# Global attention: where the results are normalised and where the row maxima are split and turned

## The reference

```
scores = q @ k.T / sqrt(8)          # per head, 1024 x 1024
attn   = softmax(scores, axis=-1)
out    = attn @ v
```

## Time and profile before

| what | value |
|---|---|
| three runs | 3819.56, 3825.5, 3826.06 us (median 3825.5) |
| profiled execution, device time | 3821.91 us |
| its span, first to last instruction | 3820.1 us |
| mean granted TensorE clock | 0.987 |
| busy share of the whole span | PE 96%, DVE 84%, ACT 75%, POOL 63% |
| global attention within the span | about 61 us to 750 us |

### The profile page before, as it was taken

How to read it: one execution, slowest core, us unless ns; L and a number is a source line. 1 busy time by engine, 2 the same in 40 slices (tenths; PEclk the granted TensorE clock), 3 DMA queues, 4 the chain that set the end, 5 groups by cost and what they waited for, 6 DMA issues and landing times. The chain is left out here.

```text
span 3820.1 us, 161411 instructions
## 1 busy us (share of the span) xinstructions
PE 3661.5 (96%) x70604; PEld 2660.4 (70%) x70604; DVE 3217.1 (84%) x4678; ACT 2863.7 (75%) x5074; POOL 2397.6 (63%) x1986
## 2 busy tenths in 40 slices
PE   6999999959999999999999999999999999999997
PEld 2222222247888888888888888888888888888885
DVE  7999999668888888888888888888888888888884
ACT  3888888857777777777777777777777777777774
POOL 3100000077777777878777777778777777778783
PEclk8999999989999999999999999999999999999999
DMA  3110000034444344433444344444444443444432
GB/s 117 38 39 21 20 22 18 7 95 109 110 112 106 104 122 113 111 107 104 119 115 112 105 106 116 120 110 105 106 116 116 111 106 105 127 117 109 108 105 57
DMA packets 202568, 360.17 MB, mean 94 GB/s; under 512 B 35522, under 2 KB 74054, under 8 KB 201542
## 3 DMA queue, kind: packets, MB, share of 16 engines
q1 hardware_dynamic: 201802, 348.76, 34.3%
HBM read 236.73 MB, written 111.67 MB: 91 GB/s over the span
## 5 line engine op out<-in xcount | busy, mean ns | idle before, releaser
L1202 POOL TENSOR_TENSOR T<-T 128x1024 f32<-128x1024 f32 x384 | 909.2, 2380 | 25.9 <-DVE T L1681 25.1
L1220 POOL TENSOR_TENSOR T<-T,rn 128x1024 f32<-128x1024 f32 x384 | 732.0, 1907 | 27.1 <-POOL rn L1213 0.4
L1292 PE MATMUL PA<-Wqkv,XS 128*128 128x512 f32 x2304 | 633.4, 410 | 11.4 <-DVE XS L1642 8.2
L787 ACT ACTIVATE E<-p_low 128x512 f32<-128x512 f32 x1024 | 556.2, 597 | 114.6 <-PE p_low L637 100.5
L716 DVE TENSOR_REDUCE negmax<-p_max 128x1 f32<-128x1024 f32 x512 | 588.9, 1215 | 19.7 <-PE p_max L616 19.7
L1292 PEld LDWEIGHTS PA<-Wqkv,XS 128*128 128x128 f32 x2304 | 414.7, 193 | 81.9 <-DVE XS L1642 11.2
L1689 DVE TENSOR_REDUCE ss<-SQ 128x32 f32<-128x2048 f32 x192 | 436.9, 2275 | 0.0
L1368 PE MATMUL PB<-ET,VW 64*64 64x32 f32 x24576 | 399.6, 220 | 16.8 <-DVE T L1681 8.8
L1368 PEld LDWEIGHTS PB<-ET,VW 64*64 64x64 f32 x24576 | 377.5, 135 | 54.8 <-DVE T L1681 28.6
L1320 PE MATMUL PD<-ident,T 128*128 128x128 f32 x3072 | 409.5, 276 | 6.3 <-POOL T L1220 5.3
L1381 PEld LDWEIGHTS PD<-Wo,OT 128*128 128x128 f32 x3072 | 365.9, 192 | 61.3 <-issue 61.1
(11 more groups left out here) (165 smaller groups left out, 6718.8 us busy)
## 6 DMA issues: line engine op xcount, KB each, us to landing
VW<-v_rows SPq DMA_DIRECT2D x768, 256.0 KB, 4.5
v_rows<-Vs SPq DMA_DIRECT2D x192, 512.0 KB, 6.0
Wraw<-in_Wqkv SPq DMA_DIRECT2D x40, 192.0 KB, 5.1
QA<-parts_q SPq DMA_DIRECT2D x384, 16.0 KB
KA<-parts_k SPq DMA_DIRECT2D x192, 32.0 KB
parts_q<-AO SPq DMA_DIRECT2D x8, 384.0 KB, 2.7
parts_k<-AO SPq DMA_DIRECT2D x8, 384.0 KB, 3.3
Wo<-in_Wo SPq DMA_DIRECT2D x12, 256.0 KB, 4.8
```

The costliest lines, as they stand in the source:

```text
L787: act.activation(E[:, s % 4, c, :], p_s[:, (64 * g + i) % NS, :], ACT.Exp, scale=DH ** -0.5)\
L1202: pool.tensor_tensor(out=t_, in0=t_, in1=T2[:, i * HALF:(i + 1) * HALF], op=ALU.add).then_inc(ad.sem, 1)
L1220: pool.tensor_tensor(out=t_, in0=t_, in1=rn[:, p, i * LH:(i + 1) * LH].unsqueeze(2).broadcast_to([P, LH, LD]), op=ALU.mult).then_inc(no.se ...
L1292: mm = pe.matmul(pair[:, half, :], XS[:, b, i, 1:P + 1], Wqkv[:, l % 2, j, lo:lo + 512], start=(k == 0), stop=(k == 2))
```

## The change

- `max_rows`: DVE now makes the two bfloat16 parts from the columns (`nmc`, 128 x 16 each), directly behind the sixteenth reduction. PE transposes both parts in bfloat16 into one bank of the score ring, and ACT copies the 16 x 256 rows to `nmb`. SP's DMAs wait for ACT.
- `result`: PE transposes into a bank of the score ring. ACT copies the bank (128 x 512) back to OE; POOL raises the sums to the power -1 and multiplies into AO. `result_copy` now waits for POOL's product of the group before (s_ao).
- The three score banks are numbered by `ring`: scores, rows and results in one list. p_max holds units alone.
- Rows move from steps 5 and 13 to 4 and 12, between scores 1 and 2; units from five steps of two to four (24 are done ahead of group 0, where there were 22); `late` goes.
- At the start PE's wait for `s_lo` and `s_va` of the opening stands ahead of `max_rows(0, 0)`.

```diff
     def units(g, s):
-        if s < 5:
-            return [(g, 1, 6 + 2 * s + i) for i in range(2)]
+        if s < 4:
+            return [(g, 1, 8 + 2 * s + i) for i in range(2)]
         if g + 1 == NG:
             return []
-        if s < 13:
-            return [(g + 1, 0, 2 * (s - 5) + i) for i in range(2)]
-        return [(g + 1, 1, 2 * (s - 13) + i) for i in range(2)]
+        if s < 12:
+            return [(g + 1, 0, 2 * (s - 4) + i) for i in range(2)]
+        return [(g + 1, 1, 2 * (s - 12) + i) for i in range(2)]
...
     def on_pool(pool):
+        def result(g, qh):
+            b, hg = divmod(g, HG)
+            o = OE[:, qh, :].rearrange("p (q c w) -> p q c w", q=4, w=VW)
+            pool.wait_ge(s_ex.sem, s_ex.at(RING["result", g, qh]))
+            pool.tensor_tensor(out=rsum[:, qh, :, :], in0=o[:, :, :, DH], in1=minus[:, :, :], op=ALU.pow)\
+                .then_inc(s_rc.sem, 1)
+            pool.wait_ge(s_rc.sem, s_rc.at(g, qh + 1))
...
+            pool.tensor_tensor(out=a[:, :, hg, :, :], in0=o[:, :, :, 0:DH],
+                               in1=rsum[:, qh, :, :].unsqueeze(3).broadcast_to([P, 4, GH, DH]),
+                               op=ALU.mult).then_inc(s_ao.sem, 1)
...
             pool.tensor_copy(VG[:, g % 2, :, :, 0:DH + 1], VA[:, g // HG, :, heads(g), :]).then_inc(s_vg.sem, 1)
+            if g >= 2:
+                result(g - 2, 1)
+            if g >= 1:
+                result(g - 1, 0)
...
+        result(NG - 2, 1)
+        result(NG - 1, 0)
+        result(NG - 1, 1)
...
     def on_pe(pe):
         def max_rows(g, qh):
-            k = TURN["rows", g, qh]
-            pe.wait_ge(s_mr.sem, s_mr.at(k - 1))
-            pe.transpose(p_max[0:GH * 4, k % 2, 0:P], negmax[:, qh, :, :].rearrange("p c q -> p (c q)"),
-                         ident[:, :]).then_inc(s_mx.sem, 1)
+            n = RING["rows", g, qh]
+            pe.wait_ge(s_mb.sem, s_mb.at(g, qh + 1))
+            if n >= NS:
+                pe.wait_ge(s_ex.sem, s_ex.at(n - NS))
+            for j in range(2):
+                mm = pe.transpose(p_s[0:GH * 4, n % NS, :].bitcast(BF16)[:, j * P:(j + 1) * P], nmc[:, qh, j, :],
+                                  w["ident_b"][:, :])
+            mm.then_inc(s_st.sem, 1)
...
         def result(g, qh):
-            k = TURN["result", g, qh]
+            n = RING["result", g, qh]
             pe.wait_ge(s_oe.sem, s_oe.at(g, qh + 1))
-            pe.wait_ge(s_mr.sem, s_mr.at(k - 2))
+            pe.wait_ge(s_ex.sem, s_ex.at(n - NS))
             for qt in range(4):
-                mm = pe.transpose(p_max[:, k % 2, qt * P:(qt + 1) * P], OE[:, qh, qt * P:(qt + 1) * P], ident[:, :])
-            mm.then_inc(s_mx.sem, 1)
+                mm = pe.transpose(p_s[:, n % NS, qt * P:(qt + 1) * P], OE[:, qh, qt * P:(qt + 1) * P], ident[:, :])
+            mm.then_inc(s_st.sem, 1)
...
     def on_dve(dve):
         def max_rows(g, qh):
-            k = TURN["rows", g, qh]
-            dve.wait_ge(s_mx.sem, s_mx.at(k))
+            dve.wait_ge(s_mr.sem, s_mr.at(TURN["unit", g, qh, HU - 1]))
             if g > 0:
-                dve.wait_ge(s_md.sem, s_md.at(g - 1, 64 * (qh + 1)))
-            rows = p_max[0:GH * 4, k % 2, 0:P]
-            dve.tensor_copy(nmb[:, qh, 0, :], rows).then_inc(s_mb.sem, 1)
-            dve.wait_ge(s_mb.sem, s_mb.at(g, qh + 1))
-            dve.tensor_tensor(out=nmb[:, qh, 1, :], in0=rows, in1=nmb[:, qh, 0, :],
-                              op=ALU.subtract).then_inc(s_mr.sem, 1)
+                dve.wait_ge(s_st.sem, s_st.at(RING["rows", g - 1, qh]))
+            columns = negmax[:, qh, :, :].rearrange("p c q -> p (c q)")
+            dve.tensor_copy(nmc[:, qh, 0, :], columns).then_inc(s_nc.sem, 1)
+            dve.wait_ge(s_nc.sem, s_nc.at(g, qh + 1))
+            dve.tensor_tensor(out=nmc[:, qh, 1, :], in0=columns, in1=nmc[:, qh, 0, :],
+                              op=ALU.subtract).then_inc(s_mb.sem, 1)
...
     def on_act(act):
         def result_copy(g, qh):
             act.wait_ge(s_pv.sem, s_pv.at(g, 8 * (qh + 1)))
             if g > 0:
-                act.wait_ge(s_mx.sem, s_mx.at(TURN["result", g - 1, qh]))
+                act.wait_ge(s_ao.sem, s_ao.at(g - 1, qh + 1))
...
+        def max_rows(g, qh):
+            n = RING["rows", g, qh]
+            act.wait_ge(s_st.sem, s_st.at(n))
+            if g > 0:
+                act.wait_ge(s_md.sem, s_md.at(g - 1, 64 * (qh + 1)))
+            act.activation(nmb[:, qh, :, :].rearrange("r j n -> r (j n)"),
+                           p_s[0:GH * 4, n % NS, :].bitcast(BF16)[:, 0:2 * P], ACT.Copy).then_inc(s_ex.sem, 1)
+
+        def result(g, qh):
+            n = RING["result", g, qh]
+            act.wait_ge(s_st.sem, s_st.at(n))
+            act.activation(OE[:, qh, :], p_s[:, n % NS, :], ACT.Copy).then_inc(s_ex.sem, 1)
+
+        max_rows(0, 0)
         for g in range(NG):
             for s in range(16):
                 for c in range(GH):
-                    i = 4 * s + c
-                    act.wait_ge(s_st.sem, s_st.at(g, i + 1))
+                    if s == 4 and c == 2:
+                        max_rows(g, 1)
+                    if s == 12 and c == 2 and g + 1 < NG:
+                        max_rows(g + 1, 0)
...
+                if s == 3 and g > 0:
+                    result(g - 1, 1)
+                if s == 11:
+                    result(g, 0)
...
         result_copy(NG - 1, 1)
+        result(NG - 1, 1)
```

More of the change, by code:

```diff
@@ L473, in global_attention @@
     s_mr = m.count("s_mr")
+    s_nc = m.count("s_nc", 2)
     s_mb = m.count("s_mb", 2)
     s_md = m.count("s_md", 128)
-    s_st = m.count("s_st", 64)
-    s_ex = m.count("s_ex", 64)
+    s_st = m.count("s_st")
+    s_ex = m.count("s_ex")
+    s_ao = m.count("s_ao", 2)
+    s_mi = m.count("s_mi")
     s_pv = m.count("s_pv", 16)
@@ L523, in turns, with ring, add @@
                 todo = units(g, s)
[L524 to L527, removed]
+                for u in todo:
+                    add("unit", *u)
+        return at
+    TURN = turns()
+    def ring():
+        at = {}
+        def add(kind, *key):
+            at[(kind, *key)] = len(at)
+        add("rows", 0, 0)
+        for g in range(NG):
+            for s in range(16):
+                add("score", g, s, 0)
+                add("score", g, s, 1)
+                if s == 4:
                     add("rows", g, 1)
-                if s == 13 and g + 1 < NG:
+                if s == 12 and g + 1 < NG:
                     add("rows", g + 1, 0)
[L531 to L534, removed]
+                add("score", g, s, 2)
+                add("score", g, s, 3)
                 if s == 3 and g > 0:
@@ L540, in turns @@
         return at
-    TURN = turns()
+    RING = ring()
     def on_sp(sp):
@@ L547, in load @@
             if g >= 3:
-                sp.wait_ge(s_st.sem, s_st.at(g - 3))
+                sp.wait_ge(s_st.sem, s_st.at(RING["score", g - 3, 15, 3]))
             for u in range(2):
@@ L554, in max_rows @@
         def max_rows(g, qh):
-            sp.wait_ge(s_mr.sem, s_mr.at(TURN["rows", g, qh]))
+            sp.wait_ge(s_ex.sem, s_ex.at(RING["rows", g, qh]))
             for j in range(2):
@@ L581, in on_pool @@
     def on_pool(pool):
+        def result(g, qh):
[5 more added lines that the diff above has]
+            pool.wait_ge(s_rc.sem, s_rc.at(g, qh + 1))
+            if g == 0 and qh == 0:
+                for u in range(2):
+                    for i in range(2):
+                        pool.wait_ge(s_pd[u][i].sem, s_pd[u][i].at(B - 1))
+            a = AO[:, b, 4 * qh:4 * qh + 4, :].rearrange("p q (g c d) -> p q g c d", g=HG, d=DH)
+            pool.tensor_tensor(out=a[:, :, hg, :, :], in0=o[:, :, :, 0:DH],
+                               in1=rsum[:, qh, :, :].unsqueeze(3).broadcast_to([P, 4, GH, DH]),
+                               op=ALU.mult).then_inc(s_ao.sem, 1)
+        pool.memset(minus[:, :, :], -1.0).then_inc(s_mi.sem, 1)
+        pool.wait_ge(s_mi.sem, 1)
         pool.wait_ge(w["vz"].sem, 1)
@@ L647, in weigh @@
                 lo, hi = 256 * halves[0], 256 * (halves[-1] + 1)
-            pe.wait_ge(s_ex.sem, s_ex.at(g, 4 * s + 4))
+            pe.wait_ge(s_ex.sem, s_ex.at(RING["score", g, s, 3]))
             if s == 0:
@@ L670, in on_pe @@
             max_unit(*u)
+        pe.wait_ge(s_lo.sem, s_lo.at(CHUNKS - 1))
+        pe.wait_ge(s_va.sem, s_va.at(CHUNKS - 1))
         max_rows(0, 0)
@@ L673, in on_pe @@
             max_unit(*u)
-        pe.wait_ge(s_lo.sem, s_lo.at(CHUNKS - 1))
-        pe.wait_ge(s_va.sem, s_va.at(CHUNKS - 1))
         for g in range(NG):
@@ L678, in on_pe @@
                 todo = units(g, s)
-                late = s % 8 == 5
                 w_ = (g, s - 1) if s > 0 else (g - 1, 15) if g > 0 else None
                 score(g, s, 0)
-                if todo and not late:
+                if todo:
                     max_unit(*todo[0], (0,))
                 score(g, s, 1)
-                if todo and not late:
```

(26 more changed lines are left out.)

24 lines of the change are left out of this document (5 added, 19 removed).

## The result

The changed kernel takes 3783.0 us (median of four runs, 3781.8 to 3787.8), the kernel before 3822.5 in the same comparison: ratio 0.9903, 95% interval 0.9882 to 0.9924. The forecast was 3789 against 3825.5, a ratio of 0.9905. The recorded ratio is not the quotient of these two medians (that is 0.9897), and its interval is 0.002 wide on each side: that forecast and result agree to 0.0002 is luck, that they agree within the interval is not. The profiled execution took 3781.8, its span is 3780.0.

The account below looks back on a forecast made before the run. DVE was taken to bind by 2% with PE directly behind; PE's terms gave 19.25 us a half-group instead of 20.67. 42.6 + 0.2 - 2.7 - 3.85 - 2.0 = 34.3 saved, so 3789 us; own range 3780 to 3798.

Parts of the forecast that it names:

- The bound: Global attention before the change: DVE binds at 2.26 us a step, by 2%, with PE directly behind at 2.21.
- Rival 1: DVE stays the bound after the change: half-group 18.6 to 18.8, 3770 us at 18.65; chance 0.15.
- rival 2: Score ring makes ACT the bound: copies delay PE by 0.8 a half-group, not 0.21; 3806 us; chance 0.13.
- Rival 3: Slower: rows transpose in PE's queue waits for DVE's parts and the ring, holding score 2; 3833 us; chance 0.05.
- each 0.1 costs 0.1: PE's wait for DVE's row parts: none, by a margin of 0.2 us; any lateness beyond that costs its full length.
- PE's sum: PE's half-group: eight steps 17.68, result copy 0.48, result transposes 0.59, rows 0.21, late score 0.21; 19.17 us.
- The 0.08 for DVE holding PE: Runs of units: DVE falls back 0.05 us a step against PE and may hold it; 0.08 added, giving 19.25.
- The ring: Three score banks at step 4: ACT's two new copies make score 3 0.21 us late; bounds 0 and 0.9.
- Paid once: Costs outside the repeating half-groups: start 2.7 us, end 3.85, ACT's weight copy in groups 2 to 4 2.0.
- The result costs 0.78: DVE's timeline before the change: a hole of 0.78 us a half-group at the result.
- the rows' hole: DVE's timeline before the change: the rows cost 1.70 us a half-group; after it 0.5, bounds 0.3 and 0.7.

Follow-up runs that it names:

- the pair twice: Changed kernel with DVE's cast and subtraction of the rows made twice, the first into a spare tile: 19.14 us a half-group, as in the changed kernel.
- the rows alone with the pair twice: Kernel before with only the rows' part of the change, results left on DVE, and DVE's cast and subtraction of the rows made twice: 19.52 us a half-group.
- The rows alone: Kernel before with only the rows' part of the change, results left on DVE through p_max: 19.15 us a half-group, ratio 0.9890 to the kernel before.

## Why the prediction was right

- *The bound.* That DVE leads by 2% and PE stands behind it at 2.21 a step held: the changed kernel runs at PE's terms, and taking 0.33 from PE or adding 0.4 to DVE moved it by 0.32 and by 0. Rival 1 (19.14 against 18.65) and rival 2 (0.26 of ring, not 0.8) fell. Rival 3 fell too: PE comes to DVE's parts 0.3 behind their end. But the price that went with it, "each 0.1 costs 0.1", was wrong: with the pair twice PE waited 0.17 for the parts, at no cost.
- *PE's sum.* 17.68 + 0.48 + 0.59 + 0.21 + 0.21 came within 0.03 of 19.14. That is closer than its terms: the rows on PE were 0.14 and not 0.21, the late score 0.26 and not 0.21, the result copy 0.44 and not 0.48, and these errors cancel. The 0.08 for DVE holding PE has no counterpart: steps of units run at 2.21.
- *The ring.* The walk through step 4 (exponential 0 at 0.60, score 3 late by 0.21, measured 0.26) is confirmed from both sides: rows and result apart, -0.17; ACT's copy doubled, +0.49. What it took for an effect of both copies is about half due to the rows alone, which stayed with 0.14 when the result's copy was a step away.
- *Paid once.* Start 2.64 for 2.7, in part by luck: in five other traces with the same code up to there the first score came at 89.9 to 90.9, against 89.88 here, and in two others with the start of the kernel before at 87.0 and 87.8. The clock rose later too, 0.50 until 97.5 us and not 95.0, and the first half-group lost 0.4 more than before; that moment lay between 96.9 and 104.1 in those traces, so the 0.4 is one draw. The end 3.5 for 3.85: the power cost 2.91, between the bounds of 1.0 and 4.1, and 0.4 below the price per element that the sum took. The 2.6 cycles per element of the Trainium skill (GPSIMD Engine Reference, Elementwise — side-by-side cycle accounting) were measured on an addition; by them the end would have been 1.6, an estimate, and the measurement decides.
- *Wrong in the reading, though not in the sum.* "The result costs 0.78" was read as DVE's price. The runs showed that DVE's 0.54 of work there cost nothing, and that moving the results is worth 0.34 alone and nothing beside the rows, less 3.5 at the end. It did no harm because the gain was not summed from DVE's holes but from PE's floor. By the prices of the prediction, the rows' hole alone carries DVE to 20.67 - 1.70 + 0.5 = 19.47, within 0.3 of PE's 19.17; it measured 19.15. So the question whether the results had to move at all could have been asked from the same rows.

## What to carry to other kernels

When the second engine stands 2% behind the first, price the change by the second one's own terms, taken from a stretch where it alone runs, and test each half of a change against that floor: here one half reached it alone, and the other only moved work. A hole in an engine's timeline is not the price of the work that lies in it; look at which buffer the next item needs and when it came free. In a short ring of buffers the first copies may cost less than their length (here 0.26 for two of 0.48 and some 0.27), but behind them nothing is left: one more of 0.48 cost 0.49. And what hides in such a wait is free: 0.17 of lateness on DVE cost nothing.

## What was not expected of the hardware

With POOL's power twice, 2.5 us in which PE waited for ACT's copy (up to 214.4) were followed by a granted clock of 0.50, the lower of the two levels (1.2 GHz), between about 215.5 and 219, though PE was busy again. The same followed the other two waits, from 256.5 to 263.3 and from 300.8 to 304.3. The three waits of 2.5 cost 3.9, 5.1 and 3.7, the most where the clock stayed low longest. So a wait on PE cost up to twice its length here.

POOL's power took 1.02 us for 128 x 4 and 2.91 for 128 x 16; from these two, an estimate: 0.16 per element of a partition and some 0.4 once.

DVE's small operations between SBUF tiles can last as long as POOL's beside them. In the rows alone with the pair twice, three of the four ran beside POOL's products of 128 x 512 (1.25 each) in one half-group, and took 1.17 to 1.19 instead of 0.17, each until POOL's product was done:

```profile
136.27 9.87 POOL L617 TENSOR_TENSOR X<-X,mod 128x512 f32<-128x512 f32 x8
...
143.77 1.19 DVE L750 CAST nmc<-negmax 128x16 bf16<-128x16 f32 x1
```

PE waited 2.7 for the parts, the granted clock was 0.50 from 147.5 to 150.9 behind that, and the half-group took 23.92 instead of 19.5. The rows alone met it once, with one operation of 1.19 (a half-group of 20.03). Beside POOL's power the same operations took their usual 0.17 to 0.18, 48 times in the changed kernel with the pair twice. In the changed kernel none of them fell beside a product of 128 x 512: that is a matter of where they happen to lie, and the prediction had not asked. What makes the difference between POOL's product and its power no run tested.
